# A fused image filter, text encoder and window-attention kernel: the first block's loads and VectorE order are changed, and the feed-forward residual moves from GpSimd to ScalarE and to another place among TensorE's products

## The reference

```
h  = layernorm(h + attention(h) @ wc) * g1 + e1
ff = relu(h @ w1 + b1) @ w2 + b2
h  = layernorm(h + ff) * g2 + e2
```

## Time and profile before

| | us |
|---|---|
| median of 3 runs (1001.42 to 1001.96) | 1001.82 |
| profiled execution, its own time | 999.17 |
| span of the profiled execution | 997.3 |
| PE busy | 905.2 (91%) |
| DVE busy | 834.9 (84%) |
| ACT busy | 699.3 (70%) |
| POOL busy | 122.3 (12%) |

### The profile page before, as it was taken

The page is one execution under the profiler, slowest core; times in us unless marked ns, Lnnn a source line. Parts: engine busy times, 40 slices in busy tenths (PEclk is TensorE's granted clock), DMA queues, the critical chain, the costliest instruction groups (busy, mean ns, idle before and its releaser), DMA issues.

```text
span 997.3 us, 18874 instructions
## 1 busy us (share of the span) xinstructions
PE 905.2 (91%) x6960; PEld 700.2 (70%) x6960; DVE 834.9 (84%) x1160; ACT 699.3 (70%) x2252; POOL 122.3 (12%) x147
## 2 busy tenths in 40 slices
PE   5489999999999999999999997889998999999997
PEld 4267777777777777777777775767675766667675
DVE  2999999999999999999999998987899599352443
ACT  2666876976877877877876875757767686767842
POOL 6201011011011011101101111101010111000000
PEclk9699999999999999999999999999998999999999
DMA  7311120031010121010220010000001000100000
GB/s 173 113 35 28 66 89 19 22 122 45 18 45 17 32 90 39 17 46 14 70 80 11 17 38 11 12 22 12 27 17 38 17 22 17 44 27 2 17 1 32
DMA packets 24925, 39.00 MB, mean 39 GB/s; under 512 B 4001, under 2 KB 20609, under 8 KB 23553
## 3 DMA queue, kind: packets, MB, share of 16 engines
q1 hardware_dynamic: 24448, 36.74, 11.6%
q0 software_dynamic: 384, 1.05, 0.5%
HBM read 22.21 MB, written 5.24 MB: 28 GB/s over the span
## 4 chain that ended last, share of the span: by engine, by line
DVE 47%; PE 25%; ACT 16%; issue 9%; DMA 2%; POOL 1%; SPq 0%; DVEq 0%; POOLq 0%; ACTq 0%
ACT prob L1086 7%; PE ps_t L849 7%; DVE f L1726 4%; DVE f L1753 4%; PE ps_m L860 4%; DVE f L1748 4%; DVE p L1738 4%; DVE f L1757 4%; DVE neg_max L1762 4%; DVE f L1743 3%; ACT u L1073 3%; DVE f L1721 2%; DVE f L1710 2%; PE ps_s L796 2%; DVE f L1699 2%
## 5 line engine op out<-in xcount | busy, mean ns | idle before, releaser
L1086 ACT ACTIVATE prob<-ps_s,neg_max 128x128 f32<-128x128 f32 x512 | 181.3, 408 | 7.3 <-DVE neg_max L1762 7.3
L1086 ACT ACTIVATION_READ_ACCUMULATOR prob<-ps_s,neg_max 128x1 f32 x512 | 126.6, 249 | 0.0
L655 PE MATMUL ps_t<-w,hidT 128*128 128x256 f32 x512 | 125.7, 383 | 0.0
L1094 ACT ACTIVATE probT<-ps_t 128x512 f32<-128x512 f32 x128 | 81.1, 634 | 44.3 <-PE ps_t L601 28.7
L655 PEld LDWEIGHTS ps_t<-w,hidT 128*128 128x128 f32 x512 | 91.1, 190 | 12.1 <-ACT hidT L1168 3.0
L849 PE MATMUL ps_t<-km,w_fc 128*128 128x384 f32 x256 | 93.9, 503 | 1.0 <-ACT km L1282 1.0
L601 PE MATMUL ps_t<-ident,prob 128*128 128x128 f32 x512 | 81.5, 283 | 12.9 <-ACT prob L1086 6.7
L601 PEld LDWEIGHTS ps_t<-ident,prob 128*128 128x128 f32 x512 | 60.0, 144 | 36.6 <-issue 14.7
L1762 DVE TENSOR_REDUCE neg_max<-ps_s 128x8 f32<-128x1024 f32 x64 | 77.5, 1211 | 4.6 <-PE ps_s L591 4.6
L1341 ACT ACTIVATE prob<-ps_s,neg_max 128x128 f32<-128x128 f32 x192 | 53.8, 376 | 22.6 <-DVE neg_max L1935 22.2
L849 PEld LDWEIGHTS ps_t<-km,w_fc 128*128 128x128 f32 x256 | 47.5, 195 | 26.8 <-issue 3.7
(11 more groups left out here) (179 smaller groups left out, 2038.9 us busy)
## 6 DMA issues: line engine op xcount, KB each, us to landing
w<-in_w SPq DMA_DIRECT2D x8, 1024.0 KB, 5.0
u<-u SPq DMA_DIRECT2D x80, 63.0 KB
p<-p SPq DMA_DIRECT2D x80, 63.0 KB
w_attn<-in_w_attn SPq DMA_DIRECT2D x4, 768.0 KB, 5.4
out<-w SPq DMA_DIRECT2D x7, 384.0 KB, 2.5
o_all<-in_o SPq DMA_DIRECT2D x4, 512.0 KB, 3.7
filtered<-f_out SPq DMA_DIRECT2D x4, 512.0 KB, 3.2
x<-filtered SPq DMA_DIRECT2D x8, 256.0 KB, 2.8
```

Of the source, the lines that this page charges most:

```text
L655: last = mm(ps_t[:, 0, D * t:D * t + D], hidT[:, m, P * t:P * t + P], w2[:, m], start=False, stop=(m == MC - 1), skip_group_check=True)
L1086: last = A(prob[:, n % 2, hh], ps_s[n % 2][:, hh], ACT.Exp, scale=-1.0, bias=neg_max[:, n % 2, hh:hh + 1], accum_out=den)
L1094: A(probT[:, 4 * half:4 * half + 4].rearrange("p h k -> p (h k)"), ps_t[:, 1], ACT.Copy).then_inc(s["act_pT"], 1)
```

## The change

- SP: the first images are loaded right behind the tokens, the field's four DMAs come ahead of the q/k/v weights, in two semaphores (`l_vf` for columns, `l_vf_rows` for rows).
- PE, ACT, SP and DVE wait at the start for eight constants only (N_EARLY), not for the zeroing of `v`.
- POOL waits for the q/k/v weights (`l_qkv`) between the second and the third gather. The window masks are 128 wide, not 4 x 128, and are read with a broadcast.
- DVE: `first_step` has another order. The head mask, the first column difference and its product come ahead of the positions; `flux_cols(0)` comes ahead of the first maximum, the pair masks behind image step 0, `head_max(0, 2)` behind `columns_apart(1)`, and the two `normalise` calls between the divergence instructions of step 1.
- The residual of the feed-forward part: `carry_bias` moves from POOL to ACT, as two ACTIVATEs of 128x256 with the bias `b2`, behind the last exponentials and ahead of `probs_out(a, 2, 0)`. `carry_ffn` moves on PE from ahead of `ff2` part 0 to behind part 5 and `turn_probs(a, 2, 1)`. Part 0 now starts the bank and waits for the third hidden part.

```diff
@@ sync
+            load_images(0).then_inc(s["l_img"], 16)
             (taps, pe)
-            load_images(0).then_inc(s["l_img"], 16)
+            for comp, loaded in ((1, "l_vf"), (0, "l_vf_rows")):
+                for img in range(2):
+                    sp.dma_start(vf[64 * img:64 * img + 64, comp], d["vf"][comp].rearrange("(p r) c -> p r c", r=RPP)).then_inc(s[loaded], 16)
             sp.dma_start(w_attn[:, :, 0:3 * D], d["w_attn"][0][:, :, 0:3 * D]).then_inc(s["l_qkv"], 16)
-            for img in range(2):
-                for comp in range(2):
-                    sp.dma_start(vf[...], ...).then_inc(s["l_vf"], 16)
...
-            sp.wait_ge(s["c_pool"], N_CONST)
+            sp.wait_ge(s["c_pool"], N_EARLY)
@@ gpsimd
                 if b == 1:
                     const(pool.memset(v[:], 0.0))
                     assert c == N_CONST
+                    pool.wait_ge(s["l_qkv"], 16)
...
-            def carry_bias(k):
-                pool.wait_ge(s["act_hF"], k + 1)
-                if k:
-                    pool.wait_ge(s["pe_ff2"], k)
-                if k < LAST:
-                    pool.wait_ge(s["dve_div"], sum(BLOCK_ITERS[:k + 1]) + 1)
-                b2 = cols[:, k // PAIRS, 2].unsqueeze(2).to_broadcast([P, KC, D])
-                pool.tensor_tensor(hT_r[:], hT_f[:], b2, ALU.add).then_inc(s["pool_hr"], 1)
@@ tensor, block_step
                 ff1(f, 3)
-                carry_ffn(f)
                 ff2(f, range(0, 1))
                 attend(a, 1)
                 ff2(f, range(1, 2))
                 turn_probs(a, 2, 0)
                 ff2(f, range(2, 6))
                 turn_probs(a, 2, 1)
+                carry_ffn(f)
                 ff2(f, range(6, 7))
@@ tensor, fuse_first: carry_ffn(LAST) moves from ahead of ff2 part 0 to ahead of part 6
@@ scalar
+            def carry_bias(k):
+                act.wait_ge(s["act_hF"], k + 1)
+                if k:
+                    act.wait_ge(s["pe_ff2"], k)
+                for c in range(KC):
+                    last = A(hT_r[:, c], hT_f[:, c], ACT.Identity, bias=cols[:, k // PAIRS, 2, c:c + 1])
+                last.then_inc(s["act_hR"], 1)
...
                 exps(a, 3, 1)
+                carry_bias(f)
                 probs_out(a, 2, 0)
@@ vector, first_step
+                head_pairs()
                 columns_apart(0)
                 columns_weighed(0)
-                head_max(0, 0)
+                positions_first()
                 rows_apart(0)
                 advance_columns(0)
                 rows_weighed(0)
                 advance_rows(0)
                 flux_rows(0)
+                flux_cols(0)
+                head_max(0, 0)
+                divergence_columns(0)
                 head_max(0, 1)
-                flux_cols(0)
-                divergence_columns(0)
                 divergence_rows(0)
                 divergence_both(0)
                 divergence_out(0)
-                head_max(0, 2)
+                row_pairs()
                 positions_rest()
                 columns_apart(1)
+                head_max(0, 2)
                 head_max(0, 3)
...
                 divergence_columns(1)
+                normalise(0, 0)
                 divergence_rows(1)
+                normalise(0, 1)
                 divergence_both(1)
                 divergence_out(1)
-                normalise(0, 0)
-                normalise(0, 1)
```

More of the change, by code:

```diff
@@ L541, in project, with carry @@
                 return last
-            def carry(bank, src):
+            def carry(bank, src, first):
                 for t in range(2):
@@ L546, in carry @@
                         at = D * t + P * c
-                        mm(bank[:, at:at + P], src[:, c, P * t:P * t + P], ident[:], start=(t + c == 0), stop=False, skip_group_check=True)
+                        mm(bank[:, at:at + P], src[:, c, P * t:P * t + P], ident[:], start=(first and t + c == 0), stop=False, skip_group_check=True)
             def carry_attn(k):
@@ L551, in carry_attn @@
                     pe_.wait_ge(s["act_ff1"], 4 * k)
-                carry(row_bank, hT_a[:, k % 2])
+                carry(row_bank, hT_a[:, k % 2], True)
             def carry_ffn(k):
-                pe_.wait_ge(s["pool_hr"], k + 1)
-                pe_.wait_ge(s["act_ff1"], 4 * k + 3)
-                carry(ps_t[:, 0], hT_r)
+                pe_.wait_ge(s["act_hR"], k + 1)
+                carry(ps_t[:, 0], hT_r, False)
             def keys(k, g):
@@ L652, in ff2 @@
                     if t == 0:
-                        pe_.wait_ge(s["act_ff1"], 4 * k + part + 1)
+                        pe_.wait_ge(s["act_ff1"], 4 * k + max(part + 1, 3))
                     for m in range(2 * (part % 4), 2 * (part % 4) + 2):
-                        last = mm(ps_t[:, 0, D * t:D * t + D], hidT[:, m, P * t:P * t + P], w2[:, m], start=False, stop=(m == MC - 1), skip_group_check=True)
+                        last = mm(ps_t[:, 0, D * t:D * t + D], hidT[:, m, P * t:P * t + P], w2[:, m], start=(part == 0 and m == 0), stop=(m == MC - 1), skip_group_check=True)
                 if part == 7:
@@ L785, in tile_scores @@
                     pe_.wait_ge(s["f_k"], n + 1)
-                    m = mask[:, 1].rearrange("p a k -> p (a k)")
+                    m = mask[:, 1].unsqueeze(1).to_broadcast([P, 4, P])
                     for hb in range(2):
-                        mm(quad[hb], ident_h[:], m, start=True, stop=False, skip_group_check=True)
+                        mm(quad[hb].rearrange("p (a k) -> p a k", a=4), ident_h[:], m, start=True, stop=False, skip_group_check=True)
                 for c in range(FKV):
@@ L1139, in keys_out @@
             def keys_out(k, g):
+                if k == 0:
+                    act.wait_ge(s["c_heads"], 1)
                 act.wait_ge(s[f"pe_k{g}"], k + 1)
@@ L1346, in tile_mask @@
                 for hb in range(2):
-                    last = A(quad[hb], mask[:, 0].rearrange("p a k -> p (a k)"), ACT.Copy)
+                    last = A(quad[hb].rearrange("p (a k) -> p a k", a=4), mask[:, 0].unsqueeze(1).to_broadcast([P, 4, P]), ACT.Copy)
                 last.then_inc(s["f_mask"], 1)
@@ L1669, in _, with head_pairs, row_pairs, positions_first @@
                     dve.sem_inc(s["gen_free"], 1)
-            dve.wait_ge(s["c_pool"], N_CONST)
-            tick(dve.tensor_reduce(head_mask[:], ident[:].rearrange("p (j o d) -> p o j d", o=2, d=TKD), AX.XY, ALU.add))
-            for r in range(4):
-                tick(dve.tensor_reduce(row_mask[:, r:r + 1], ident[:, 32 * r:32 * r + 32], AX.X, ALU.add))
-            dve.wait_ge(s["chain"], chain[0])
-            link(tt(pair_mask[:], row_mask[:, 0:2], row_mask[:, 2:4], ALU.add))
-            ts(pair_mask[:], pair_mask[:], SCALE_F, None, ALU.mult).then_inc(s["c_scaled"], 1)
-            dve.wait_ge(s["c_scaled"], 1)
-            pe_rows = pe[:].unsqueeze(1)
-            dve.wait_ge(s["g_emb_first"], 32)
-            dve.wait_ge(s["l_pe"], 16)
-            tt(h[:, 0:2], h[:, 0:2], pe_rows.to_broadcast([P, 2, D]), ALU.add).then_inc(s["h_ready"], 1)
+            dve.wait_ge(s["c_pool"], N_EARLY)
+            pe_rows = pe[:].unsqueeze(1)
+            def head_pairs():
+                dve.tensor_reduce(head_mask[:], ident[:].rearrange("p (j o d) -> p o j d", o=2, d=TKD), AX.XY, ALU.add).then_inc(s["c_heads"], 1)
+            def row_pairs():
+                for r in range(4):
+                    tick(dve.tensor_reduce(row_mask[:, r:r + 1], ident[:, 32 * r:32 * r + 32], AX.X, ALU.add))
+                dve.wait_ge(s["chain"], chain[0])
+                link(tt(pair_mask[:], row_mask[:, 0:2], row_mask[:, 2:4], ALU.add))
+                ts(pair_mask[:], pair_mask[:], SCALE_F, None, ALU.mult).then_inc(s["c_scaled"], 1)
+                dve.wait_ge(s["c_scaled"], 1)
+            def positions_first():
+                dve.wait_ge(s["g_emb_first"], 32)
+                dve.wait_ge(s["l_pe"], 16)
+                tt(h[:, 0:2], h[:, 0:2], pe_rows.to_broadcast([P, 2, D]), ALU.add).then_inc(s["h_ready"], 1)
             def positions_rest():
```

36 lines of the change are left out of this document (18 added, 18 removed).

## The result

| | before | after |
|---|---|---|
| median of the runs compared, us | 1001.89 (1001.42 to 1003.13) | 1039.17 (1037.24 to 1044.57) |
| ratio, 95% interval | | 1.0381 (1.0345 to 1.0418) |
| profiled execution, its own time | 999.17 | 1037.69 |
| span | 997.3 | 1036.0 |
| mean granted TensorE clock | 0.976 | 0.955 |

The kernel is slower, as forecast, but by 37.3 us and not by 22.0; 1039.17 lies outside the range of 1009 to 1030.

What follows compares the result with a forecast made beforehand. DVE was taken to bound blocks 1 to 15. Text blocks 18.9, fusion 1.0 and start 2.1 sum to 22.0 us; on the profiled 999.17 that is 1021.2, and 2.65 up to the median gives 1023.8, range 1009 to 1030.

Steps and rivals of the forecast that it cites:

- The stop in a text block: Blocks 1 to 14: DVE stops 1.35 us per block at `moments_ffn`, not given back, 18.9 us in all.
- PE's margin ahead of the transposition: Text block, ahead of `turn_probs(a, 2, 1)`: 0.28 us, or 0.24 after the signal, to absorb a later ACT copy.
- The ScalarE estimate of 1.02 for the pair: ACT's two bias ACTIVATEs by the skill's budget: 1.65 us per block, 4.2 more in all; not used.
- block 15's margin: Block 15, ahead of the moments: 2.46 us of margin cover the whole delay, so only 14 blocks count.
- rival E: Text blocks: clock falls to 1.2 GHz behind PE's wait, 53 us more, 1077 us; chance 0.05.
- The start: Up to block 1's first column difference: DVE waits for the halo, block 1 at 61.7, a loss of 2.1 us.
- the time of the halo: At the start: `p1` halo lands behind six weight loads, so DVE starts `divergence_rows(0)` at 33.5, against 35.52 before.
- The fusion: `fuse_first`: ACT's pair costs nothing, the moved matmuls add 1.0 us (0.5 to 1.2).
- A: Start keeps its gain, `divergence_rows(0)` some 9 us earlier than forecast: start -6.9, time 1014.8 us; chance 0.15.
- C: Start keeps its gain and ACT's pair costs nothing on the path: sum 2.9, time 1004.7 us; chance 0.06.
- B: Text blocks: ACT's pair costs nothing, only the moved matmuls do, 0.63 us a block; time 1013.7 us; chance 0.08.
- D: Faster: start gains 6.9 us, DVE's stop at `moments_ffn` under 0.42 a block; 997.3 us at 0.1; chance 0.08.

Runs made afterwards that it cites:

- Experiments 3: Against the kernel before, only PE's eight identity matmuls moved behind the sixth product and transposition, bias left on POOL: 1014.06 us, ratio 1.0104.
- experiment 4: `act_pair`: kernel before plus two ACTIVATEs of 128x256 with bias ahead of `probs_out(a, 2, 0)`, result unread: 1011.57 us, ratio 1.0072.
- experiment 7: Against the residual part of the change alone, sixteen identity transpositions added in PE's wait ahead of `turn_probs(a, 2, 1)`: 1024.82 us, 1.0222 to the kernel before.
- 8: Against the kernel before, bias moved to ACT behind the third `hidden_out`, ahead of the tanh; matmuls in their old place: 1002.83 us, ratio 1.0011.
- 12: `carry_first`: residual part of the change alone, but with the moved matmuls ahead of `turn_probs(a, 2, 1)`: 1014.03 us, 1.0115 to the kernel before.
- experiment 5: Against the start part of the change alone, first halo issued ahead of SP's gather wait and six weight loads: 1000.35 us, 0.9987 to the kernel before.
- resid_only: Against the kernel before, only the residual part of the change (bias on ACT, identity matmuls moved), start as before: 1032.33 us, ratio 1.030.

## Why the prediction was right and wrong

**The stop in a text block: the mechanism right, the size by sizes that erred against each other.** The chain was as forecast: ACT's pair, its copy, the transposition, the moved matmuls, the last part, the moments. Experiments 3 and 4 show its two causes one by one. A block loses 1.45, against the forecast's 1.35. The stop in the bracket, 1.36, leaves out the 0.09 of lost overlap and only looks like a hit. The pair takes 0.80 of the path and not the 0.72 that I read from the pair of `hidden_out`. PE's margin ahead of the transposition is 0.13 and not 0.24: PE starts 0.15 behind the end of ACT's copy, where I had taken 0.04, so 0.28 - 0.15 is left. The transposition takes 0.47 up to the next matmul behind a wait, against 0.44 before, and the eight matmuls take 136.61 - 135.72 = 0.89 and not 1.00. Together 0.80 - 0.13 + 0.03 + 0.89 - 0.13 = 1.46. The sum over the blocks then agreed, 19.0 against 18.9, by luck: 14 x 1.45 is 20.3, and some 1.3 came back in the two blocks that had been longer before. The ScalarE estimate of 1.02 for the pair (the Trainium skill, ScalarE: Activation LUTs, Rules for kernel authors) is its duration in the trace, 1.02, but the next instruction starts 0.80 behind its start, and the path sees only that. That the time is not given back, and that block 15's margin covers it, was right.

**The clock: wrong, 6.6 us in the blocks and about 2.7 in the fusion.** The step that failed is rival E as an all-or-nothing case with a chance of 0.05. I took one row with 2 us without work at a granted clock of 1.00 as the answer for fourteen repetitions, and put the clock at nothing in the sum. The same 2.08 us wait brought the clock down in four blocks and left it up in seven. The price was wrong too: the clock came back before the last parts were done (0.93 from 100 to 101), so such a block loses 1.67 and not 3.8. That the wait is the cause is shown by experiment 7, in which filling it took the 3.0 stops away, by 3, 4, 8 and 12, whose waits are shorter or absent and which have none, and by the count over all traces. Why one wait of 2.08 is followed by a fall and the next is not stays open. In the fusion the clock's part is a reading of windows, not an experiment. From the start of its image step to the end of the span the fusion takes 378.1 us before and 382.6 after, but 384.6 in `act_pair`, whose fusion is that of before, line for line. So the stage differs by several microseconds with nothing changed in it, and one trace of each kernel can't tell this change's share from that. How much of the 2.7 this change would cost on average stays open.

**The start: wrong by 6.5.** The forecast had the right place (the row divergence, waiting for the halo) and the right reason (the halo's place in SP's order), and from there on the sum held: 68.21 - 39.48 = 28.7 against 28.2. The step that failed is the time of the halo, 39.48 against 33.5, which is 6.0 of the 6.5. Its terms:
- the q/k/v weights let POOL go on at 15.26, where I had taken 12.5 for their landing on the ground that "the same bytes go ahead of them": +2.8
- POOL's issues: 23.04 - 15.26 = 7.8 from the third gather to the last against 6.3, because the first two issues behind the wait took 1.98 and 1.42 and not 0.95 each: +1.5
- SP went on 3.9 later, as estimated (4), and its six loads took 3.2 against the estimated 3.15
- from the last load's issue to the halo 39.48 - 30.16 = 9.3 against 7.3: +2.0, with its own issue at 31.23 among it, which I had left out.

These are 6.3 and not 6.0, because the forecast had a slip of 0.3 the other way: 12.5 + 6.3 is 18.8 and not 19.1. Its 7.3 isn't exact either: 30.0 lies 7.0 behind the end of the last issue, 22.54 + 0.43.

The question whether the halo waits behind the loads ahead of it is settled as far as its place goes. It took 39.48 - 31.23 = 8.2 us from its issue to its use, the DMA engines were full until it came, and experiment 5 removed the whole wait by its place alone. Windows of after (the last number but one is the share of the DMA engines, the number before it the granted clock):

```profile
38.00:39.00 1.00, 0.50 0.90 265
39.00:40.00 1.00, 0.50 0.42 168
```

The rule that each DMA engine takes the descriptors of one issuing engine in ring order (the Trainium skill, DMA: Bandwidth & Descriptors, Queues, rings and completion order) agrees with this trace. No run here tells a strict order from a mere sharing of full engines, since the early halo of experiment 5 met neither.

**The fusion: the term was right.** The moved matmuls cost 1.00, forecast 1.0. The rest of the 4.4 is what goes with the clock (2.7) and 0.7 in small steps that I did not trace.

**The other rivals.** A and C fell with the start. B fell with experiment 4: the pair alone does make a stop of 0.48. D asked for a stop under 0.42 us, and it is 1.36.

The missing 16.7 us of span (38.7 - 22.0) are thus 6.5 of the start, 6.6 + 2.7 of the clock, and 0.9 of small terms.

## What to carry to other kernels

Where an engine never pauses, write down by how little its next operand is early (here 0.13 us), and move neither an instruction from ahead of a wait to behind it (0.89 us of matmuls) nor one ahead of a copy that others wait for (0.80). A small transfer that the bound engine needs goes ahead of bulk loads in its queue, and a wait that delays these loads delays all that is issued behind them. A new wait on TensorE is to be priced twice, for itself and for a granted clock that may fall behind it in a part of the repetitions; harmless work in the wait, or the work exchanged across it as in `carry_first`, is worth a try. And one trace in which such waits passed without a fall, as before's four, does not say that the next one will.

## What the runs showed of the hardware

- Eleven equal waits of 2.08 us ahead of equal work were followed by a granted clock of 0.50 in four blocks and by 1.00 in seven, in `resid_only` and in the full change, in different blocks. Over all traces a fall followed 42 of 85 waits of 1.87 to 2.40 us and none of 192 waits of 0.7 to 1.72, and took 1.7 us of TensorE's work each time.
- Sixteen useless transpositions in each of these waits made a kernel some 6 us faster.
- The same code for the fusion took 378.1 us in one kernel and 384.6 in another. The kernel before alone took 998.35 to 1009.89 us in 22 executions of one series, at a mean granted clock of 0.974 in the fastest and 0.964 in the slowest.
- PE started 0.15 us behind the end of the ACT copy that it waited for, and DVE 0.04 behind the end of PE's last part.
- An indirect DMA's issue on POOL, 0.95 us in most, took 1.98 and 1.42 in the first two behind the landing of the q/k/v weights. Why is not shown.
- Two ACTIVATEs of 128x256 with a bias from SBUF hold ACT for 0.80 us up to the next start, with a duration of 1.02; the pair from PSUM took 0.72 and 0.86.
